# Attention weighted values: one key tile on four query halves in place of two key tiles on two query chunks, in 32 short steps

## The reference, cut to what matters

```python
qkv = x @ w_qkv + b_qkv                      # x is (1, 4096, 256) after a layer norm
scores = einsum('bqhd,bkhd->bhqk', q, k) * D ** -0.5      # 16 heads, D = 16
attn = softmax(scores, axis=-1)
out = einsum('bhqk,bkhd->bqhd', attn, v).reshape(B, N, C)
return out @ w_proj + b_proj
```

## Time and profile before

| | before |
|---|---|
| median of 3 runs | 3294.21 us (3290.62 to 3294.38) |
| the profiled execution's own time | 3291.98 us |
| its span in the profile | 3290.2 us |
| granted PE clock, mean share of full speed | 0.965 |
| PE busy | 3136.5 us (95%) |
| DVE busy | 2824.3 us (86%) |
| ACT busy | 2514.8 us (76%) |
| POOL busy | 262.0 us (8%) |

### The profile page before, as it was taken

The page is one execution under the profiler, slowest core; times in us unless marked ns, Lnnn a source line. Parts: engine busy times, 40 slices in busy tenths (PEclk is TensorE's granted clock), DMA queues, the critical chain, the costliest instruction groups (busy, mean ns, idle before and its releaser), DMA issues.

```text
span 3290.2 us, 80364 instructions
## 1 busy us (share of the span) xinstructions
PE 3136.5 (95%) x27243; PEld 1406.9 (43%) x27243; DVE 2824.3 (86%) x3108; ACT 2514.8 (76%) x4551; POOL 262.0 (8%) x810
## 2 busy tenths in 40 slices
PE   8799999999999999999999999999999999988983
PEld 3444443444344434444444344434444444456662
DVE  5389998999899989998999899989999999456666
ACT  6158888888888888888888888888888888733333
POOL 2300000000000000000000000000000000011113
PEclk9689999999999999999999999999999999989996
DMA  7700101010110001010101010101010101000001
GB/s 255 90 1 1 30 11 27 14 27 14 21 21 21 21 18 24 18 24 15 27 11 30 8 33 8 33 5 37 5 37 5 36 1 30 1 0 0 0 0 51
DMA packets 27384, 83.26 MB, mean 25 GB/s; under 512 B 4641, under 2 KB 15633, under 8 KB 24018
## 3 DMA queue, kind: packets, MB, share of 16 engines
q1 hardware_dynamic: 26818, 77.84, 10.7%
q0 software_dynamic: 272, 1.05, 0.1%
HBM read 57.90 MB, written 20.97 MB: 24 GB/s over the span
## 4 chain that ended last, share of the span: by engine, by line
PE 94%; DVE 2%; issue 2%; ACT 1%; DMA 1%; POOL 1%; DVEq 0%; SPq 0%; POOLq 0%; ACTq 0%
PE ps L1023 41%; PE ps L1034 35%; PE ps L1253 4%; PE ps L998 3%; PE ps L1044 2%; PE ps L1202 2%; PE ps L957 2%; PE ps L1242 1%; PE ps L1177 1%; PE ps L971 1%; PE ps L1052 1%; PE ps L949 1%; DMA q_stack<-qk_parts 1%; ACT q_raw L619 1%; PE ps L1219 0%
## 5 line engine op out<-in xcount | busy, mean ns | idle before, releaser
L750 DVE TENSOR_REDUCE partial<-ps 128x1 f32<-128x1024 f32 x2048 | 2460.7, 1223 | 202.5 <-PE ps L998 158.5
L569 ACT ACTIVATE work<-ps 128x512 f32<-128x512 f32 x4096 | 2203.9, 598 | 383.0 <-PE ps L1023 173.9
L998 PE MATMUL ps<-k_stack,q_stack 48*128 48x512 f32 x4096 | 1509.4, 449 | 25.3 <-DMA q_stack<-qk_parts 17.0
L1023 PE MATMUL ps<-q_stack,k_stack 64*128 64x512 f32 x4096 | 1508.2, 448 | 18.8 <-issue 17.8
L1034 PE MATMUL ps<-work,v_head 128*32 128x256 f32 x16384 | 1304.4, 393 | 0.0
L1023 PEld LDWEIGHTS ps<-q_stack,k_stack 64*128 64x128 f32 x4096 | 633.0, 185 | 814.4 <-ACT work L569 695.6
L998 PEld LDWEIGHTS ps<-k_stack,q_stack 48*128 48x128 f32 x4096 | 622.6, 187 | 55.6 <-DVE partial L750 31.9
L1034 PEld LDWEIGHTS ps<-work,v_head 128*32 128x32 f32 x16384 | 330.9, 108 | 702.6 <-issue 436.8
L415 POOL CAST nm_parts<-negmax 128x4 bf16<-128x4 f32 x128 | 24.7, 193 | 2256.1 <-DVE negmax L757 2255.2
L1253 PE MATMUL ps<-k_raw,q_raw 128*128 128x256 f32 x512 | 126.3, 403 | 17.8 <-ACT q_raw L619 17.8
L619 ACT ACTIVATE q_raw<-ps 128x1024 f32<-128x1024 f32 x32 | 32.8, 1024 | 131.4 <-PE ps L1242 131.4
(11 more groups left out here) (128 smaller groups left out, 1137.4 us busy)
## 6 DMA issues: line engine op xcount, KB each, us to landing
k_stack<-qk_parts SPq DMA_DIRECT2D x96, 256.0 KB, 4.2
q_stack<-qk_parts SPq DMA_DIRECT2D x96, 256.0 KB, 4.2
qk_parts<-qk_part SPq DMA_DIRECT2D x32, 512.0 KB, 2.8
x_sb<-L_attn_x SPq DMA_DIRECT2D x8, 512.0 KB, 11.1
out<-work SPq DMA_DIRECT2D x8, 512.0 KB, 2.9
k_raw<-L_ffn_aux_values SPq DMA_DIRECT2D x1, 1024.0 KB
work<-L_attn_w_qkv POOLq DMA_DIRECT2D x1, 768.0 KB, 7.4
q_raw<-L_ffn_aux_keys SPq DMA_DIRECT2D x1, 512.0 KB
```

What stands on the lines that cost most here:

```text
L569: act.activation(probs[:, g % DEPTH, i, :], ps[:, bank, :], ACT.Exp, scale=SCALE).then_inc(exp_done, 1)
L750: dve.tensor_reduce(partial[:, k // 4, k % 4:k % 4 + 1], ps[:, 2 * slot:2 * slot + 2, :], AX.XY, ALU.max).then_inc(max_used, 1)
L998: last = pe.matmul(ps[:, 2 * slot + e, :], q_stack[HALF:HALF + ROWS, b1, c * CH + (k // 4) * P:c * CH + (k // 4 + 1) * P], k_stack[HALF:HA ...
L1023: pe.matmul(ps[:, bank, :], k_stack[0:HALF, b, P * tile:P * (tile + 1)], q_stack[0:HALF, b, at:at + CH], start=True, stop=True).then_inc(s ...
```

## The change

One block of weighted values is now one key tile on four query halves. The group i of partitions holds the queries of half `i % 2` of chunk `i // 2`, all four with the same tile g. So every group sums all key tiles, the accumulator is 256 columns wide instead of 512 on the same 128 partitions, and nothing is left for the combine to add: `sel` has 4 x 17 columns instead of 2 x 17, and the combine is two matmuls of 68 columns instead of four of 34. ACT's copy at L592 (now of 256 columns) is half as wide.

With one tile to a block, the 16 units become 32 equal steps of two scores, one piece (two M matmuls), and four PV matmuls; each step is score, M, score, M, PV. The number of scores, exponentials, M matmuls, reductions and PV matmuls stays what it was, and so do their sizes. The lag (`LAG` = 2) and the ring of `probs` (`DEPTH` = 4) are now counted in steps and so are half as long in time. `probs` takes half the room. PV of steps 0 and 1 both stand behind step 3. The combine stands behind step 7, which holds piece 15, instead of behind half unit 9, which holds piece 17. The maximum rows, loads and the steps of the last iteration stand where they stood, counted in half units.

```diff
-    KG = NT // 2
+    KG = NT
-    PVH = CH // 2
+    QH = CH // 2
-    ROW_UNITS = (7, 14)
-    COMB_UNIT = 4
-    COMB_AFTER = LEAD + 2 * COMB_UNIT + 1
+    ROW_STEPS = (15, 29)
+    COMB_STEP = 7
+    COMB_AFTER = LEAD + COMB_STEP
-    LOAD_EVERY = 2
+    LOAD_EVERY = 4
...
-        o_sb = sb("o_sb", [P, CH])
+        o_sb = sb("o_sb", [P, QH])
-        sel = sb("sel", [P, 2 * (D + 1)])
+        sel = sb("sel", [P, 4 * (D + 1)])
...
-                act.activation(o_sb[:, :], ps[:, O_BANK, :], ACT.Copy).then_inc(o_evac, 1)
+                act.activation(o_sb[:, :], ps[:, O_BANK, 0:QH], ACT.Copy).then_inc(o_evac, 1)
...
+            def weighted_values(g, it, b):
+
+                pe.wait_ge(exp_done, it * (2 * KG) + (2 * g + 2 + CREDIT[exp_done]))
+                if g == 0:
+                    pe.wait_ge(o_evac, it + 1)
                 for i in range(4):
-                    last = pe.matmul(ps[32 * i:32 * i + 32, O_BANK, cols], v_head[:, b, 2 * g + i % 2, :],
-                                     probs[:, g % DEPTH, i, cols], start=(g == 0 and half == 0), stop=(g == KG - 1 and half == 1))
-                if half == 1:
-                    last.then_inc(pv_done, 1)
+                    last = pe.matmul(ps[32 * i:32 * i + 32, O_BANK, 0:QH], v_head[:, b, g, :],
+                                     probs[:, g % DEPTH, i // 2, QH * (i % 2):QH * (i % 2 + 1)],
+                                     start=(g == 0), stop=(g == KG - 1))
+                last.then_inc(pv_done, 1)
...
-                for i in range(TPC):
-                    last = pe.matmul(ps[:, bank, 64 * i:64 * i + 2 * (D + 1)], o_sb[:, P * i:P * (i + 1)], sel[:, :],
+                for i in range(2):
+                    last = pe.matmul(ps[:, bank, P * i:P * i + 4 * (D + 1)], o_sb[:, P * i:P * (i + 1)], sel[:, :],
                                      start=True, stop=True)
...
+            def step(g, it, b, j, ahead, before):
+
+                turn = j % 2
+                p = LEAD + g
+                since_comb = p - COMB_AFTER - 1
+                for a in range(2):
+                    score(g, a, it, b, j, bool(ahead))
                     if p // 16 < len(ahead):
+                        if since_comb == 1 and a == 0:
+                            pe.wait_ge(comb_used, it + 1 + CREDIT[comb_used])
+                        max_half(p % 16, a, it * 2 + (AHEAD + p // 16), *ahead[p // 16],
+                                 (p + turn + (since_comb >= 0)) % 2, since_comb)
+                if before:
+                    weighted_values(*before)
...
                 for g in range(LAG, KG):
-                    unit(g, it, b, j, ahead, (g - LAG, it, b))
-                    if g == COMB_UNIT:
+                    step(g, it, b, j, ahead, (g - LAG, it, b) if g > LAG + 1 else None)
+                    if g == LAG + 1:
+                        weighted_values(0, it, b)
+                        weighted_values(1, it, b)
+                    if g == COMB_STEP:
```

109 lines of the change are left out of this document (41 added, 68 removed).

## The result

| | before | after |
|---|---|---|
| median of 6 runs each | 3294.38 us (3290.62 to 3295.13) | 3268.05 us (3264.68 to 3276.26) |
| ratio | | 0.9924, 95% interval 0.9912 to 0.9937 |
| the profiled execution's own time | 3291.98 us | 3264.68 us |
| its span | 3290.2 us | 3262.9 us |
| granted PE clock | 0.965 | 0.967 |

The changed kernel is 0.76% faster, about 25 us (21 to 29 by the interval). The forecast was 3262 us with a range of 3245 to 3280. The time lies inside it, 6 us above the forecast.

The account below looks back on a forecast made before the run. PE was taken to bound the kernel, with 94% of the span. Copy 13.7 + combine 17.0 + ends 1.1 = 31.8 us off 3291.98 gave 3260.2; with 2.2 for the median, forecast 3262 us, range 3245 to 3280.

Parts of the forecast that it names:

- The copy: Steps 2 and 3: narrower accumulator copy shortens the pair from 2.84 to 2.60 us, 57 x 0.24 = 13.7 us gained.
- the copy holds ACT for 0.48 us: Unit 2 before the change: ACT's copy starts at 1498.75, the exponential follows at 1499.23; the new copy holds ACT 0.27.
- the copy costs the same whatever its width, 0: Lower bound on the gain from ACT's narrower accumulator copy: 0; the upper bound was 15.4 us.
- the narrow copy holds ACT as long as before: Rival at ACT's accumulator copy: its gain stays away, 3276 us; one form of a case given 17% in all.
- The combine: Four weight loads fewer save 0.44 us; a slot wait leaves 0.27 us, x 63 iterations = 17.0 us gained.
- the two rules weighed in the prediction: Combine's small matmuls: 60 cycles overhead each, saving only 0.09 us, against weight loads of 107 ns; the trace's 0.11 favoured loads.
- Steps instead of units: PE's order: 32 steps of score, M, score, M, PV cost 1.23 us each as before; price 0.
- DVE behind the combine: Reading values and `negmax` packed between pieces 15 and 16 fit by 0.1 us; price 0, if missed 6 us.
- the rival of a slower kernel: PV blocks cost more with one tile on four groups and the same 256 columns: 3313 us, 7%.
- Ends: Last iteration's combine and the one after shrink 0.44 each, the last wait for the copy 0.2: 1.1 us gained.
- a spread of some 3 us: Loop returns: a slow stretch more or less at one or two of them, some 3 us.

Follow-up runs that it names:

- experiment 1: The changed kernel with ACT's inner loop over the first three iterations of a head written out: 3260.20 us, ratio 0.9903 to the kernel before.
- experiment 2: The kernel before with ScalarE's inner loops over a head's iterations written out, nothing else: 3291.05 us, ratio 0.9997.
- experiment 3: The changed kernel with ACT reading the 256 accumulator columns twice and writing 512: 3278.07 us, ratio 0.9952 to the kernel before.
- Experiment 4: The changed kernel with each matmul of the combine issued twice, behind step 7 as before: 3277.95 us, ratio 0.9953 to the kernel before.
- experiment 6: The changed kernel with the combine moved from behind step 7 to behind step 3: 3263.44 us, ratio 0.9900 to the kernel before.
- experiment 7: The changed kernel with the combine behind step 3 and ACT's inner loop written out: 3257.74 us, ratio 0.9896 to the kernel before.
- experiment 8: The changed kernel, ACT's loops written out, VectorE's loop nested, combine behind step 3 but behind step 7 in one iteration of eight: 3245.06 us, ratio 0.9850.
- experiment 9: The changed kernel, ACT's loops written out, VectorE's loop nested, combine behind step 3 in every iteration: 3255.15 us, ratio 0.9898 to the kernel before.
- experiment 5: The changed kernel with score, M, M, score in odd steps instead of score, M, score, M: 3265.22 us, ratio 0.9920 to the kernel before.

## Why the prediction held, and where it did not

**The copy: a term mis-sized, 13.7 forecast, 6.0 measured.** The step of the prediction that failed is "the copy holds ACT for 0.48 us", read as the copy's own cost from the earlier trace rows. The distance of 0.48 us was a maximum of two things: the copy, and in the second and third iteration of a head the turn of ACT's loop. The slope taken from the two copies was right, 0.27 forecast and 0.26 measured where no turn stands between. Where one does, the distance fell to 0.45 to 0.49 only (0.37 to 0.39 in the last two heads). The prediction asked which engine is late next, found PE at 0.27, and did not ask what else of ACT lies under the copy. Experiments 1 to 3 show it from three sides: written out it gives 5.2 us more in steps 2 and 3, 11.2 with the 6.0; on the kernel before it gives nothing there; and with a wide copy the whole gain of steps 2 and 3 is gone. The smaller part is that 2.60 became 2.64: the fourth score's weights load 1.20 us behind the opening (733.44 - 732.24 in experiment 1), 1.19 forecast; PV starts 0.44 behind that, 0.42 forecast; and from there to the next step it is 1.00, as forecast, with 0.01 us of rounding. Its own bound, "the copy costs the same whatever its width, 0", covered this half of the iterations by another cause, and so did its rival that the narrow copy holds ACT as long as before.

ScalarE's fixed cost shows here too. The Trainium skill, ScalarE: Activation LUTs, section What ACT_TABLE_LOAD costs, led to an estimate of 0.31 us for the new copy; the trace has 0.26 and decides, so the slope through the two copies was the better guide.

**The combine: 17.0 forecast, 14.7 measured** (63 x 0.234). The mechanism was right and its size slightly off: 3.31 in place of 3.28, since the reduction of piece 15 started 0.80 us behind the opening (741.68 - 740.88), not 0.77, and 3.54 in place of 3.55 before. The weight load of piece 16 stands 0.26 us behind the score, forecast about 0.25. Experiment 4 shows that the wait binds, experiments 6 to 9 that it goes where the reduction is hidden (steps 7 and 8 and the combine cost 3.05 us together there, in place of 3.31).

On the price of a small matmul the two rules weighed in the prediction are decided. Four instructions of 68 columns take 0.45 us and eight of 34 took 0.97, so the load of 128 columns sets the pace at 0.11 us. The Trainium skill, TensorE: Matmul & The Clock Gate, section LDWEIGHTS, has P / 1.2 ns for P columns, an estimate of 107 ns for these 128, and the trace agrees. The overhead of some 60 cycles that the Trainium skill, TensorEngine Tiling (Array Packing), section Instruction Overhead, gives a matmul led to an estimate of 0.09 us for the four instructions saved; the trace has 0.42, from 1.01 to 0.59 us between the combine's start and the next score.

**Steps instead of units: 0 forecast.** Steps are 1.23 us before and after, and the order inside them is worth 0.04 us an iteration (experiment 5).

**DVE behind the combine: 0 forecast, 0 measured.** The reduction of piece 16 waited for PE, not for `negmax` (743.73 above).

**PV blocks: the rival of a slower kernel fell.** 392 ns in place of 393, in the same 0.57 us of a step.

**Ends: 1.1 forecast.** From the last iteration's start to the last combine's last instruction 1.55 us went. 0.42 of them are that combine itself (below, beside 1.08 and 0.72 in the earlier trace rows), and 0.17 its wait for the copy, which fell from 0.72 to 0.55. The rest, 0.96 where the forecast had one combine's 0.44, was not taken apart.

```profile
2858.23 0.66 PE L1041 MATMUL ps<-sel,o_sb 128*128 128x68 f32 x4 [0.55 <-ACT o_sb L592]
```

**Not forecast: 6.5 us at the returns and 1.1 us in iteration 0.** Of these, 7 x 0.234 = 1.6 are the combine's. Most of the rest is time at 1.2 GHz behind the pause. At that clock a step takes 2.16 us in place of 1.23, so a microsecond spent there loses 0.43; the returns have 30.7 us of it in place of 41.0, an estimate of 4.4 us. The prediction named this as a spread of some 3 us and gave it no sign. Much of it is spread. The kernels with the return and the combine of the changed kernel (experiments 1, 3, 4 and 5) have 27.3, 37.5, 41.0 and 37.5 us at 1.2 GHz in their six returns, and the kernel before has 37.5 in experiment 2. In times these six returns are 274.7, 278.5, 280.0 (1.2 of it the combine's four instructions) and 279.4 us, between or near the 275.1 of the changed kernel and the 281.6 of before; experiment 2 has 280.6. Taken over these runs the changed return is some 3 to 4 us shorter in all, 1.4 of it the combine's, and some 3 of the 27.3 us are luck of the profiled execution.

Against the 31.8 us forecast, then, the copy brought 7.7 less, the combine 2.3 less, the ends 0.4 more, and returns and iteration 0 some 6.0 that were not forecast; the 0.8 us scattered over the ordinary steps and 0.1 outside take the sum to 27.3. The 6.0 stood in for most of what the copy did not bring. The total came closer than its largest error deserved.

## What to carry to other kernels

The distance between two instructions on an engine is the longest of all that lies between them. Before a shortened instruction is credited with its whole saving, look whether its distance to the next is the same everywhere, and what the engine does there unseen: a loop's turn is in no group of instructions. A loop turn ahead of a critical instruction can be written out.

When an instruction waits for a buffer, move it behind work that hides the wait rather than shorten what stands ahead of the wait. But judge a move in each kind of iteration: here the same move gained 0.23 us in 56 iterations and lost 16 us in seven (12 between the profiled executions of numbers 8 and 9), and only the split version kept the gain without the loss.

## What the runs showed of the hardware

**The turn of ScalarE's loop** costs about 0.45 to 0.49 us from one activation's start to the next, where two short activations without it follow each other after 0.26. In the last two heads it was 0.37 to 0.39 behind a turn, and 0.32 where the last pass leaves the loop; why is open. A copy with a distance of 0.48 us behind it hides the turn.

**The same instructions behind the last combine**, some 400 us, took 394.2 us (experiment 5) to 407.1 (experiment 3) in the profiled executions. That spread is as large as half of this change's effect, in kernels that are identical there. The granted clock goes with it, first experiment 5, then experiment 3:

```profile
2860.90:3255.20 394.30, 303.93 (x1269) 210.11 (x1268) 247.78 (x635) 143.43 (x163) 67.49 (x86) 0.90 0.03 11
```

```profile
2869.20:3276.30 407.10, 316.63 (x1269) 218.81 (x1268) 248.03 (x634) 143.21 (x163) 65.53 (x86) 0.87 0.03 11
```

PE is busy 13 us longer in the second, DVE and ACT are not. Sums against a profile should be made stretch by stretch for this reason.

**How long PE stays at 1.2 GHz behind a pause** differs from return to return within one execution, from 3.4 us to 6.8 us in the changed kernel and up to 10.2 in experiment 5. With the combine behind step 3 it was up to 13.7 us and the six iterations took up to 49.8 us in place of 45.3 to 46.4. The six returns have 61.4, 41.0 and 51.2 us at 1.2 GHz in experiments 6, 7 and 9, and 27.3 to 41.0 in the changed kernel and all experiments on it with the combine behind step 7 there. In iteration 0 the two groups lie apart: 14.9, 18.3 and 18.2 us until the clock rises with the combine behind step 3, 6.7 to 7.9 behind step 7. Why the combine's place moves that rise is open.
